# Summing pairs of state products on GpSimd before TensorE transposes them, in a selective-scan block on Trainium2

## The reference

```
h  = layernorm(x) * (1 + ca) + sa
x_ssm, z = split(h @ w_in.T + b_in);  z = silu(z)
dt = softplus(x_ssm @ w_dt.T + b_dt)
B, C = x_ssm @ w_B.T + b_B, x_ssm @ w_C.T + b_C          # 16 states each
for t:  state = exp(A * dt_t) * state + dt_t * x_t * B_t  # (channels, 16 states)
        y_t = sum over the 16 states of state * C_t
y = (y + D * x_ssm) * z;  then @ w_out, residual, layernorm, gate, a small feed-forward, gate
```

## Time and profile before

| | |
|---|---|
| median of 3 runs | 4860.93 us (4860.05 to 4862.37) |
| profiled execution, its own time | 4860.24 us |
| its span, first to last instruction | 4858.5 us |
| mean granted TensorE clock | 0.992 |
| busy: PE / PE weight loads / DVE / ACT / POOL | 96% / 65% / 77% / 79% / 69% |

### The profile page before, as it was taken

How to read it: one execution, slowest core, us unless ns; L and a number is a source line. 1 busy time by engine, 2 the same in 40 slices (tenths; PEclk the granted TensorE clock), 3 DMA queues, 4 the chain that set the end, 5 groups by cost and what they waited for, 6 DMA issues and landing times.

```text
span 4858.5 us, 76453 instructions
## 1 busy us (share of the span) xinstructions
PE 4659.5 (96%) x25664; PEld 3154.5 (65%) x25664; DVE 3729.6 (77%) x5163; ACT 3840.7 (79%) x6371; POOL 3365.4 (69%) x2699
## 2 busy tenths in 40 slices
PE   5899999999999999999999999999999999999998
PEld 3566666666666666666666666666666666666664
DVE  2587777887777887777787787887787787787785
ACT  0678878888888888878888878888878888878875
POOL 0476777776777776777776777776777776777774
PEclk8899999999999999999999999999999999999999
DMA  3111111111111111111111111111111111111111
GB/s 125 40 54 54 42 53 49 57 55 53 42 58 50 57 55 53 42 53 49 57 55 57 45 55 47 58 55 53 42 54 52 60 55 53 42 54 47 57 47 40
DMA packets 140649, 258.70 MB, mean 53 GB/s; under 512 B 18593, under 2 KB 18593, under 8 KB 140258
## 3 DMA queue, kind: packets, MB, share of 16 engines
q1 hardware_dynamic: 140258, 253.82, 16.4%
HBM read 216.01 MB, written 37.75 MB: 52 GB/s over the span
## 4 chain that ended last, share of the span: by engine, by line
PE 81%; DVE 7%; ACT 4%; issue 4%; POOL 1%; DVEq 0%; POOLq 0%; ACTq 0%
PE y_ps L444 16%; PE b_ps L404 16%; PE dense L536 9%; PE dense L564 9%; PE dense L597 7%; PE dense L509 6%; PE dense L404 5%; PE dense L459 3%; DVE work L1011 3%; PE dense L621 2%; PE dense L572 2%; ACT work L768 1%; ACT work L758 1%; PE dense L486 1%; DVE norm L1028 1%
## 5 line engine op out<-in xcount | busy, mean ns | idle before, releaser
L336 POOL TENSOR_TENSOR work<-work,c_bc 128x512 f32<-128x512 f32 x2048 | 2587.1, 1276 | 1275.2 <-DVE work L1011 1030.9
L1011 DVE TENSOR_TENSOR_SCAN work<-work,state,b_ps 128x512 f32<-128x512 f32 x1792 | 2256.6, 1274 | 456.5 <-PE b_ps L404 439.0
L768 ACT ACTIVATE work<-u_td,b_td 128x512 f32<-128x512 f32 x2048 | 1453.6, 710 | 258.8 <-PE b_ps L404 255.5
L444 PEld LDWEIGHTS y_ps<-ident,work 128*128 128x128 f32 x8192 | 1004.4, 141 | 778.3 <-issue 713.2
L758 ACT ACTIVATE work<-dt_t,neg_a 128x512 f32<-128x512 f32 x2048 | 1451.2, 709 | 14.5 <-DVE work L1011 14.5
L404 PE MATMUL b_ps<-ident,work 128*128 128x128 f32 x8192 | 1242.4, 274 | 43.9 <-DVE work L1011 31.9
L444 PE MATMUL y_ps<-ident,work 128*128 128x128 f32 x8192 | 1216.9, 273 | 0.0
L404 PEld LDWEIGHTS b_ps<-ident,work 128*128 128x128 f32 x8192 | 958.9, 142 | 88.2 <-DVE work L1011 52.6
L536 PE MATMUL dense<-h_t,w_in_t 128*128 128x512 f32 x1024 | 505.5, 597 | 12.6 <-ACT h_t L772 12.6
L597 PE MATMUL dense<-h_t,w_in_t 128*128 128x512 f32 x1024 | 513.6, 593 | 1.1 <-DVE u_td L1092 1.1
L509 PE MATMUL dense<-w_out_t,proj 128*128 128x512 f32 x1024 | 512.6, 593 | 0.0
(11 more groups left out here) (92 smaller groups left out, 4542.8 us busy)
## 6 DMA issues: line engine op xcount, KB each, us to landing
c_bc<-c_d SPq DMA_DIRECT2D x512, 256.0 KB, 3.2
xn<-in_x SPq DMA_DIRECT2D x128, 256.0 KB, 5.0
x<-in_x SPq DMA_DIRECT2D x128, 256.0 KB, 4.0
out_dram<-x SPq DMA_DIRECT2D x128, 256.0 KB, 2.7
work<-in_wmod SPq DMA_DIRECT2D x6, 1024.0 KB, 7.5
par_d<-work SPq DMA_DIRECT2D x4, 768.0 KB, 3.3
w_in_t<-in_w_in_t SPq DMA_DIRECT2D x1, 2048.0 KB, 15.1
gain_shift<-par_d SPq DMA_DIRECT2D x4, 512.0 KB, 4.7
```

The lines of the kernel that those rows point to most:

```text
L336: gp.tensor_tensor(pr[:, (s * U + i) % PR_RING, :], hs[:, (s * U + i) % HS_RING, :], c_bc[:, (s * N + n) % C_RING, :], ALU.mult).then_inc( ...
L444: last = mm(y_ps[:, tb, j * P:(j + 1) * P], pr[:, (s * U + i) % PR_RING, tb * P:(tb + 1) * P], ident[:, :], is_transpose=True, start=(i == ...
L768: A(v[:, n % V_RING, tb, :], u_td[:, s % 2, tb, :], ACT.Copy, scale=b_td[:, s % 2, tb, n:n + 1]).then_inc(S["v_done"], 1)
L1011: V.tensor_tensor_scan(hs[:, (s * U + i) % HS_RING, :], decay[:, (s * U + i) % DEC_RING, :], b_ps[:, i % 2, :], state[:, i:i + 1] if s % N ...
```

## The change

Four of the 16 states, n = 2, 6, 8 and 10, are *held*: their products (16 units) are not transposed into `y_ps`. After the product of the same channel group of state n+1 (3, 7, 9, 11), POOL adds the held product to it in place (`add_products`), and PE transposes the sum. So POOL gets 16 more instructions in a step, in slots 12-15, 28-31, 36-39 and 44-47, and PE gets 64 transposes less, `add_unit` of units 8-11, 24-27, 32-35 and 40-43, which would be in slots 12-15, 28-31, 36-39 and 44-47 with the new lag. Beside it: `pr` has nine buffers instead of five, LAG is 4 instead of 3, product i waits for the last reader of the buffer nine units back (a sum or a transpose), `u_td` has one buffer instead of two, and its copy on DVE now also waits until the last v of the chunk before has read it (`v_done`).

```diff
-    V_RING, DEC_RING, HS_RING, PR_RING, C_RING = 2, 6, 6, 5, 3
-    LAG = 3
+    V_RING, DEC_RING, HS_RING, PR_RING, C_RING = 2, 6, 6, 9, 3
+    LAG = 4
+
+    HELD = (2, 6, 8, 10)
...
+    def summed(n):
+        return n - 1 in HELD
...
-        u_td = sb("u_td", [P, 2, TB, D])
+        u_td = sb("u_td", [P, TB, D])
...
-                gp.wait_ge(S["y_added"], at("y_added", s, i + 1 - PR_RING))
+                k, r = (s, i - PR_RING) if i >= PR_RING else (s - 1, U + i - PR_RING)
+                if r // KD in HELD:
+                    gp.wait_ge(S["sum_done"], at("sum_done", k, sums(r + KD)))
+                else:
+                    gp.wait_ge(S["y_added"], at("y_added", k, added(r)))
...
+            def add_products(s, i):
+
+                gp.wait_ge(S["prod_done"], at("prod_done", s, i + 1))
+                gp.tensor_tensor(pr[:, (s * U + i) % PR_RING, :], pr[:, (s * U + i) % PR_RING, :],
+                                 pr[:, (s * U + i - KD) % PR_RING, :], ALU.add).then_inc(S["sum_done"], 1)
...
                         product(s, i)
+                        if summed(i // KD):
+                            add_products(s, i)
...
             def add_unit(s, i):
                 j = i % KD
+                if i // KD in HELD:
+                    return
...
+                if summed(i // KD):
+                    pe.wait_ge(S["sum_done"], at("sum_done", s, sums(i)))
...
-                    if has_s and i >= LAG + 2:
-                        if i in (LAG + 2, LAG + 3):
-                            add_unit(s, 2 * (i - LAG - 2))
-                            add_unit(s, 2 * (i - LAG - 2) + 1)
-                        else:
-                            add_unit(s, i - LAG)
+                    if has_b and i < 2:
+                        for r in ((U - 3, U - 2), (U - 1,))[i]:
+                            add_unit(b, r)
+                    if has_s and i >= LAG + 1:
+                        for r in {LAG + 1: (0, 1), LAG + 2: (2,), U - 1: (U - 5, U - 4)}.get(i, (i - LAG,)):
+                            add_unit(s, r)
...
-                A(v[:, n % V_RING, tb, :], u_td[:, s % 2, tb, :], ACT.Copy, scale=b_td[:, s % 2, tb, n:n + 1]
+                A(v[:, n % V_RING, tb, :], u_td[:, tb, :], ACT.Copy, scale=b_td[:, s % 2, tb, n:n + 1]
...
-                    V.tensor_copy(u_td[:, f % 2, tb, :], inside(s, ("z.2", "z.2", "s", "s")[tb])[:, :]
+                    dve.wait_ge(S["v_done"], at("v_done", s, (N - 1) * TB + tb + 1))
+                    V.tensor_copy(u_td[:, tb, :], inside(s, ("z.2", "z.2", "s", "s")[tb])[:, :]
```

More of the change, by code:

```diff
@@ L57, in build_program, with sums, added @@
     TOTAL += 0.8
+    def summed(n):
+        return n - 1 in HELD
+    def sums(i):
+        return sum(summed(r // KD) for r in range(i + 1))
+    def added(i):
+        return sum(r // KD not in HELD for r in range(i + 1))
     def slot(*part):
@@ L160, in build_program @@
             "SP": dict(stored_0=Q, stored_1=Q, stored_2=Q, stored_3=Q, c_stored=Q),
-            "Pool": dict(prod_done=U, xsh_done=TB, x1_done=TB, dt_done=KD, u_done=KD, sz_done=KD),
-            "PE": dict(b_made=U, y_added=U, skip_added=KD, s_ps=1, g_used=J, yz_ps=KD, out_ps=TB, res_used=TB, pre_ps=TB, xt_ps=KD, xs_ps=KD,
+            "Pool": dict(prod_done=U, sum_done=sums(U - 1), xsh_done=TB, x1_done=TB, dt_done=KD, u_done=KD, sz_done=KD),
+            "PE": dict(b_made=U, y_added=added(U - 1), skip_added=KD, s_ps=1, g_used=J, yz_ps=KD, out_ps=TB, res_used=TB, pre_ps=TB, xt_ps=KD, xs_ps=KD,
                        cb_ps=1, bt_ps=1, x2_ps=KD, dt_ps=KD, z_ps=KD, ut_ps=TB),
@@ L1041, in take_y @@
                     dve.wait_ge(S["u_done"], at("u_done", b, KD))
-                    dve.wait_ge(S["y_added"], at("y_added", b, U))
+                    dve.wait_ge(S["y_added"], at("y_added", b, added(U - 1)))
                     V.tensor_copy(y_sb[:, b % 2, tb, :], y_ps[:, tb, :]).then_inc(S["y_copied"], 1)
```

## The result

The changed kernel takes 4954.9 us (median of 4, 4951.79 to 4955.72) against 4861.0 us: ratio 1.0192, 95% interval 1.0174 to 1.0209. It is slower by 94 us; 4865 was forecast, and the range ended at 4925.

What follows compares the result with a forecast made beforehand. PE bounds a steady step, but with the sums POOL bounds product 12 to the last u. 30 steady steps x -0.05 = -1.5, first +1, last +5: 4860.9 + 4.5 = 4865 us, range 4822 to 4925.

Steps and rivals of the forecast that it cites:

- PE is the bound, a y block costs 0.44 us: Steady step: PE work fills 140.8 of 145.72 us; four transposes of one unit take 0.44 us, start to start.
- The 275 ns per transpose: PE's saving from 64 transposes: 17.6 us a step by the skill page's figure, 7.0 by starts; the starts were taken.
- A sum costs 1.37: On POOL, each sum waits for the product just ahead: 1.37 us, bounds 1.24 and 1.41; sixteen make 21.9 us a step.
- POOL becomes the bound from product 12 to the last u, and PE waits at turn_u: Stretch would need 94.0 us plus 0.1 to 0.3, against 93.8; PE waits about 5 to 6 us in slot 54.
- The tie at product 27: POOL could start product 27 at 2108.3, its scan comes at about 2108.2, with PE ahead by 0.88 us.
- my slower rival: POOL runs dry inside the stretch (0.75) and a sum costs 1.41 (0.6 a step): 4909 us, chance 0.20.
- The step that failed: Steady step: +0.3 us for the stretch from product 12 to the last u, -0.35 of old slack before turn_u: about 0.
- Ends of the run: First step with units +1 us; last step +5 us, where POOL has 17.5 us idle and gets 21.9 more.
- u_td, LAG, the ring of nine: nothing: Single u_td costs 0 (bounds 0 and 0.7 us a step); products 5 and 8 stop waiting for the ring, counted as nothing.
- Partly faster: Rival: the 51.9 us outside the stretch shrink up to 1.5 us a step, or sums start 1.24 apart: 4820 us, chance 0.20.
- PE keeps its gain: Rival: the stretch fits in 86.8 us, a sum at 0.92 us, so the 224 us are saved: 4642 us, chance 0.05.
- PE never the bound: Rival: removing transposes brings nothing and POOL's room swallows the sums, no new wait at turn_u: 4861 us, chance 0.04.

Runs made afterwards that it cites:

- runs 3 and 4: Changed kernel with only two states held, eight sums a step: 2 and 6 took 4812.6 us, 8 and 10 took 4946.1 us.
- run 5: Changed kernel with state 6 alone held, four sums a step in slots 28 to 31: 4804.4 us, ratio 0.9882 to the kernel before.
- run 1: Changed kernel with no state held, keeping the ring of nine, LAG 4 and single u_td: 4856.7 us, ratio 0.9992 to the kernel before.
- the run with the filler: Changed kernel, all four states held, plus 40 identity transposes on PE ahead of turn_u's wait for u: 4888.3 us, ratio 1.0056 to the kernel before.
- run 7: Changed kernel with states 1, 6, 8 and 13 held instead, sixteen sums a step: 4714.2 us, ratio 0.9697 to the kernel before.

## Why the prediction was wrong

- *PE is the bound, a y block costs 0.44 us*: right. State 6 alone gives back 1.76 us a step for four blocks.
- *The 275 ns per transpose of the Trainium skill (TensorE: Matmul & The Clock Gate, Part 4: PE-mode transpose) or 109 ns by starts*: the starts. The page gives 275 ns as the duration of one in another kernel, and as a duration this trace agrees (273 ns, in float32). 64 x 0.275 = 17.6 us a step has no counterpart in any run; 8 blocks gave 3.49 in the run with 6, 8 and 13.
- *A sum costs 1.37*: right. A sum starts 1.34 to 1.39 us after its product, and what follows starts 1.23 to 1.33 behind the sum.
- *POOL becomes the bound from product 12 to the last u, and PE waits at turn_u*: right in place; the matmuls waited 5.2 to 5.3 us there in a steady step, the weight load up to 6.1, where I had 5 to 6. The y blocks just ahead of it, for which I had waits of 0.9 and 0.3 us, waited under 0.2 at the matmuls, in the steps looked at. Place against number was settled by runs 3 and 4.
- *The tie at product 27*: fell the wrong way. I let PE be 0.88 us ahead there. DVE's chain of slots 9 to 17 grew by 0.3 instead, from L1048 on (run 5), PE gained nothing, and POOL ran dry for 1.17 us. The stretch got +1.01, not +0.3. This was the first half of my slower rival (0.75); its other half, a sum of 1.41, was not.
- *The step that failed*: "So a steady step is +0.3 - 0.35 = about 0." It takes the wait at turn_u as its own length and lets PE resume at the pace of before. PE resumes at half pace. That is a term of 2.27 us a step, 68 of the 94 us, and it was in no case of mine: I had looked at the clock of one step and found 1.00, in a kernel whose PE stands at most about 1.2 us at a time in such a step. Without this term the time falls inside my range: the run with the filler took 4888 us. It would still be 23 us above the forecast of 4865: with the clock up a steady step is 0.5 us longer than before (+1.01 for the stretch, -0.52 of slack), and the ends of the run cost more than I had.
- *Ends of the run*: +4.6 and +6.9, where I had +1 and +5. The first step with units has the same wait and clock as a steady one, which is most of the 4.6; 1.6 of it lie ahead of its product 12, where no sum stands yet. In the other runs that have no sum there either it comes 0.8 us earlier to 2.0 later than before, and why is open.
- *u_td, LAG, the ring of nine: nothing*: right in time, run 1. But product 8 waits for y as before; only product 5 was freed.
- *Partly faster; PE keeps its gain; PE never the bound*: all wrong for this kernel. That PE never bound is refuted by run 5: four y blocks less gave back their whole price, though PE's weight loads are busy only 65%. (The section of the Trainium skill, Perfetto Trace Analysis, Identifying the Most-Contended Engine, names MFU, the matmul work done as a share of the peak, beside the weight loads; I had used the weight loads alone.) That averages leave POOL room was true, and useless at slot 54; where idle moments of POOL follow the sums, as in run 7, 147 of the 224 us are there.

## What to carry to other kernels

Work that is moved to an engine with idle time is paid for by place: lay it against that engine's idle moments up to the next thing that the bound engine waits for, and put it where such moments follow. A wait of a TensorE that was streaming can cost more than its length, as those of 3.8 us and more did here: ask what clock comes after it, and count the work behind it at the lower level. Before an edit like this is given up, run the same number of moved instructions in another place; here that was the difference between +94 and -147 us.

## What the runs showed of the hardware

The granted clock fell at every wait of 3.8 to 5.3 us of an otherwise full PE (the changed kernel, and states 8 and 10). In the steady steps of before it stayed up at the gap of 1.2 us in slot 3 (1.6 once). The gap of 2.7 us in the run with 6, 8, 12 and 14 is between: the clock fell at 3 of 30 (at 438.7, 1158.9 and 1302.3 us) and stayed up at the others. Transposes of the identity kept it up: the run with 40 of them through the wait shows 1.00 behind it, and no fall at turn_u in any of the 30 steady steps. A four-column DVE instruction with two SBUF inputs took 0.16 us beside an idle POOL and up to 1.2 beside a busy one, always ending 0.02 to 0.03 us after POOL's instruction, while the scans kept a mean of 1.27 us in all runs. So DVE and POOL meet here at more than the semaphores.
